# Row statistics moved into the gated FFN, and three small moves in an attention's order of work

## What is computed

```
x = x + L0_xattn(layernorm(x), ctx)     # attention over channels, with a norm over a whole sample
x = x + L0_ffn(layernorm(x))            # fp8 products; gelu(x Wg) * (x Wu), then W_linear
x = x + L1_xattn(layernorm(x), ctx, ctx)
x = x + L1_ffn(layernorm(x))            # eight experts, the two best of each row, weighted by softmax
```

```
qh, kh, vh = q, k, v reshaped to (batch, head, 32, 512)     # q = layernorm(x), k = v = ctx
sm  = softmax(qh^T kh / sqrt(32))                            # 512 x 512 a head
ret = sum over l of sm[q, l] vh[:, l];  x = x + gamma * ret
```

## Time and profile before

| | us |
|---|---|
| median of 3 executions | 750.81 (748.82 to 752.76) |
| the profiled execution | 750.58 |
| its span on the core | 748.8 |
| PE busy in the span | 699.5 (93%) |
| DVE busy | 567.9 (76%) |
| ACT busy | 412.8 (55%) |
| POOL busy | 365.4 (49%) |
| mean granted TensorE clock | 0.995 |

### The profile page before, as it was taken

How to read it: one execution, slowest core, us unless ns; L and a number is a source line. 1 busy time by engine, 2 the same in 40 slices (tenths; PEclk the granted TensorE clock), 3 DMA queues, 4 the chain that set the end, 5 groups by cost and what they waited for, 6 DMA issues and landing times.

```text
span 748.8 us, 16025 instructions
## 1 busy us (share of the span) xinstructions
PE 699.5 (93%) x5065; PEld 307.8 (41%) x5093; DVE 567.9 (76%) x1109; ACT 412.8 (55%) x777; POOL 365.4 (49%) x357
## 2 busy tenths in 40 slices
PE   6999999999999999888999999989988898999995
PEld 2445444444444444322232323222224555555552
DVE  5689999796876869698889998899857565555553
ACT  2554454663646547357788877777776333222221
POOL 5666555113011031364766667776574664343433
PEclk9999999999999999999999999999999999999998
DMA  9999980017365397243344434443555899899895
GB/s 306 392 123 224 320 329 0 1 40 262 115 217 199 120 339 276 67 115 101 95 121 107 114 86 143 137 143 101 164 193 132 169 189 139 125 137 128 132 113 71
DMA packets 114189, 117.62 MB, mean 157 GB/s; under 512 B 54840, under 2 KB 78264, under 8 KB 113856
## 3 DMA queue, kind: packets, MB, share of 16 engines
q1 hardware_dynamic: 103008, 94.48, 43.9%
q0 software_dynamic: 10384, 22.02, 18.1%
q10 hardware_dynamic: 720, 0.13, 0.1%
HBM read 43.61 MB, written 59.56 MB: 138 GB/s over the span
## 4 chain that ended last, share of the span: by engine, by line
PE 17%; DMA 15%; issue 10%; DVE 9%; POOL 2%; SPq 2%; ACT 2%; POOLq 1%; DVEq 0%; ACTq 0%
DMA out<-t_room,t_tag 7%; PE l_b L1579 6%; PE ps_sm L1600 4%; DMA out<-l_pvs,t_tag 4%; DVE l_negm L1827 4%; PE l_pv L1591 3%; DMA out<-l_sums,t_tag 2%; PE l_a L1504 2%; SPq L1060 2%; DVE h_negm L1827 2%; PE l_b L1568 1%; ACT t_room L1734 1%; POOLq L1248 1%; DVE l_rst L1839 1%; DMA h_stack<-h_wide 1%
## 5 line engine op out<-in xcount | busy, mean ns | idle before, releaser
L1734 ACT ACTIVATE t_room<-l_b 128x512 f32<-128x512 f32 x256 | 139.8, 599 | 38.1 <-PE l_b L1579 34.7
L1175 PE MATMUL l_a<-w1h,h_stack 128*128 x312 | 76.5, 314 | 3.0 <-issue 1.7
L1827 DVE TENSOR_REDUCE l_negm<-l_a 128x2 f32<-128x1024 f32 x64 | 75.2, 1219 | 3.6 <-PE l_a L1504 3.1
L1204 ACT ACTIVATE l_stack<-l_stack 128x352 f32<-128x352 f32 x39 | 19.4, 498 | 105.3 <-DVE l_stack L1228 101.7
L1827 DVE TENSOR_REDUCE h_negm<-l_a 128x2 f32<-128x1024 f32 x56 | 65.9, 1220 | 4.9 <-PE l_a L1504 4.6
L1600 PE MATMUL ps_sm<-t_room,ones_f 128*32 128x512 f32 x512 | 66.6, 594 | 2.4 <-ACT l_sums L1745 2.0
L1591 PE MATMUL l_pv<-t_room,l_vt 128*32 128x512 f32 x512 | 66.5, 594 | 0.4 <-issue 0.4
L861 PE MATMUL ps_r<-f_xt,wg 128*128 128x512 fp8e4 x256 | 65.7, 379 | 0.0
L861 PE MATMUL ps_st<-f_xt,wg 128*128 128x512 fp8e4 x256 | 65.7, 379 | 0.0
L1018 POOL TENSOR_TENSOR X<-X,f_y 128x512 f32<-128x512 f32 x15 | 19.4, 1293 | 76.6 <-ACT f_y L915 76.6
L1258 POOL DMA_INDIRECT out<-t_room,t_tag x20 | 31.7, 1585 | 47.7 <-DVE t_room L1243 38.4
(11 more groups left out here) (316 smaller groups left out, 1572.0 us busy)
## 6 DMA issues: line engine op xcount, KB each, us to landing
slots_x<-empty SPq DMA_DIRECT2D x8, 2376.0 KB, 11.2
slots_x<-empty SPq DMA_DIRECT2D x7, 2112.0 KB, 17.4
h_stack<-h_wide SPq DMA_DIRECT2D x96, 64.0 KB
l_stack<-h_wide SPq DMA_DIRECT2D x96, 64.0 KB
...
```

What stands on the lines that cost most here:

```text
L1175: mm = pe.matmul(self.HP[i % 2][:, 0:self.H], T.xt[i % T.AHEAD][:, xp * self.FC + f, :], self.w1[wp][:, bass.ds(e, 1), f * self.H:(f + 1) ...
L1734: act.activation(weights_at(u, c, h)[:, :], B[t % 2][:, :], ACT.Exp, scale=SCALE).then_inc(b_ok, 1)
L1827: dve.tensor_reduce(negm[u % 2][:, 2 * half:2 * half + 2, j], A[half][:, :, :], AX.X, ALU.max, negate=True)\
```

## The change

The statistics of units 0 to 9 are computed in the FFN: those of units 0 to 3 and 4 to 7 at the end of DVE's work in the second and third group, those of 8 and 9 in the last group, at m = 0 and m = 11. mv, veps and rstd get a place for each of the 16 tiles, so a power may take several at once, and the addition of eps too. In the attention, unit u computes the statistics of unit 10 + u as long as there is one (u = 0 to 5), with POOL's power at the same place as before; the step ahead of the loop (that of unit 2) falls away, and POOL's memset of the second stack's row of ones no longer waits for it. `normalise` stands behind maxima(u+2, 1). The adding product is made as four products, each with 32 of the 128 columns of the stationary operand, into four column groups. In unit 1, SP sends the row of maxima of unit 2 ahead of that unit's values.

```diff
--- before.py
+++ after.py
@@ -938,6 +938,7 @@
                         dve.tensor_tensor(EW.w2[1][0:rows, e, cols], stage2[0:rows, cols], EW.w2[0][0:rows, e, cols], ALU.subtract)\
                             .then_inc(lo2_ok, 1)
 
+            SOON_AT = (0, 11)
             LATE = (1, 2, 3, 4, 5, 6, 9, 10, 12, 13, 14, 15)
 
             def group(g, more):
@@ -968,18 +969,24 @@
                         split(2 * g, m - (HC - 6))
                     if not more and m in LATE:
                         split(2 * g + LATE.index(m) // 6, LATE.index(m) % 6)
-                    if not more and m == 0:
-                        F.statistics(dve, X, 0)
+                    if not more and m in SOON_AT:
+                        u = (g - 1) * G + SOON_AT.index(m)
+                        dve.wait_ge(res_ok, u + 1)
+                        F.statistics(dve, X, u, u + 1)
                     if not more and m == 7:
                         F.queries(dve, X, 0)
-                    if not more and m == 11:
-                        F.statistics(dve, X, 1)
+                    if not more and m == SOON_AT[-1]:
+                        F.variances(dve, (g - 1) * G, (g - 1) * G + len(SOON_AT))
                 dve.wait_ge(h8_ok, g * HC + HC)
                 if more:
                     for part in range(6):
                         split(2 * g + 1, part)
                     if g == 0:
                         last.vector(dve, HC)
+                    else:
+                        dve.wait_ge(res_ok, g * G)
+                        F.statistics(dve, X, (g - 1) * G, g * G)
+                        F.variances(dve, (g - 1) * G, g * G)
                 else:
                     for k in range(2 * F.TC):
                         dve.wait_ge(F.a_ps, k + 1)
@@ -1001,12 +1008,12 @@
                     last.gpsimd(pool, last.batches)
                 if not more:
                     pool.wait_ge(res_ok, g * G)
+                    pool.wait_ge(F.rstd_ok, (g - 1) * G)
                     pool.memset(F.stack[F.M0:F.M0 + 1, 0, :, :], 1.0).then_inc(F.set_ok, 1)
                     pool.wait_ge(F.set_ok, 1)
-                    F.power(pool, neg_half, 0)
                     F.low_keys(pool, F.parts, 0)
                     F.low_queries(pool, F.parts, 0)
-                    F.power(pool, neg_half, 1)
+                    F.power(pool, neg_half, (g - 1) * G, F.SOONER)
                 for r in range(G):
                     if not more and r == 2:
                         F.low_keys(pool, F.parts1, 1)
@@ -1016,7 +1023,10 @@
                     pool.wait_ge(y_ok, g * G + r + 1)
                     xr = X[:, bass.ds(g * G + r, 1), :]
                     pool.tensor_tensor(xr, xr, y[r % 2][:, :], ALU.add).then_inc(res_ok, 1)
-
+                if more and g:
+                    F.power(pool, neg_half, (g - 1) * G, g * G)
+
+            assert (NG - 2) * G + 2 == F.SOONER
             groups(pool, group)
 
     return range(ops.stat_ok.num, lo2_ok.num + 1)
@@ -1025,7 +1035,9 @@
 class FirstUnit:
 
 
-    def __init__(self, nc, st, D, DH):
+    SOONER = 10
+
+    def __init__(self, nc, st, D, DH, NT):
         HU, TC = P // DH, D // P
 
         def sb(name, shape, dt=F32):
@@ -1040,7 +1052,7 @@
         parts = [self.wide[:, 2 * k * D:2 * (k + 1) * D].bitcast(BF16).rearrange("p (n d) -> p n d", d=D) for k in range(2)]
         self.parts, self.parts1 = parts
         self.kf, self.qf = self.wide[:, 4 * D:5 * D], self.wide[:, 5 * D:6 * D]
-        self.st6, self.mv, self.veps, self.rstd = sb("st6", [P, 6]), sb("mv", [P, 2]), sb("veps", [P, 1]), sb("rstd", [P, 1])
+        self.st6, self.mv, self.veps, self.rstd = sb("st6", [P, 6]), sb("mv", [P, NT, 2]), sb("veps", [P, NT]), sb("rstd", [P, NT])
         self.negm = sb("negm", [P, HU, TC])
         self.mrow = sb("mrow", [HU * TC, P], BF16)
         self.kf_ok, self.stack_ok, self.row_in, self.set_ok = sem("kf"), sem("stack0"), sem("row0"), sem("set")
@@ -1063,23 +1075,26 @@
     def place_rows(self, sp, stack, mrow, row_in):
         sp.dma_start(stack[self.M0:self.M0 + 1, 1, :, :].rearrange("o h (j t) -> o (h j) t", t=P), mrow[:, :]).then_inc(row_in, 16)
 
-    def statistics(self, dve, X, u):
-        wait(dve, self.rstd_ok, u)
-        dve.bn_stats(self.st6[:, :], X[:, u, :]).then_inc(self.stat_ok, 1)
-        wait_apart(dve, (self.stat_ok, u + 1), (self.qf_ok, u))
-        dve.bn_aggr(self.mv[:, :], self.st6[:, :]).then_inc(self.aggr_ok, 1)
-        dve.wait_ge(self.aggr_ok, u + 1)
-        dve.tensor_scalar(self.veps[:, :], self.mv[:, 1:2], EPS, None, ALU.add).then_inc(self.veps_ok, 1)
+    def statistics(self, dve, X, first, last):
+        for u in range(first, last):
+            wait(dve, self.aggr_ok, u)
+            dve.bn_stats(self.st6[:, :], X[:, u, :]).then_inc(self.stat_ok, 1)
+            dve.wait_ge(self.stat_ok, u + 1)
+            dve.bn_aggr(self.mv[:, u, :], self.st6[:, :]).then_inc(self.aggr_ok, 1)
+
+    def variances(self, dve, first, last):
+        dve.wait_ge(self.aggr_ok, last)
+        dve.tensor_scalar(self.veps[:, first:last], self.mv[:, first:last, 1], EPS, None, ALU.add).then_inc(self.veps_ok, last - first)
 
     def queries(self, dve, X, u):
         dve.wait_ge(self.rstd_ok, u + 1)
         wait(dve, self.ql_ok, u)
-        dve.tensor_scalar(self.qf[:, :], X[:, u, :], self.mv[:, 0:1], self.rstd[:, :], ALU.subtract, ALU.mult).then_inc(self.qf_ok, 1)
-
-    def power(self, pool, neg_half, u):
-        pool.wait_ge(self.veps_ok, u + 1)
-        wait(pool, self.qf_ok, u)
-        pool.tensor_tensor(self.rstd[:, :], self.veps[:, :], neg_half[:, 0:1], ALU.pow).then_inc(self.rstd_ok, 1)
+        dve.tensor_scalar(self.qf[:, :], X[:, u, :], self.mv[:, u, 0:1], self.rstd[:, u:u + 1], ALU.subtract, ALU.mult).then_inc(self.qf_ok, 1)
+
+    def power(self, pool, neg_half, first, last):
+        pool.wait_ge(self.veps_ok, last)
+        pool.tensor_tensor(self.rstd[:, first:last], self.veps[:, first:last], neg_half[:, 0:last - first], ALU.pow)\
+            .then_inc(self.rstd_ok, last - first)
 
     def high_keys(self, act, parts, u):
         act.wait_ge(self.kf_ok, 16 * u + 16)
@@ -1462,8 +1477,12 @@
             for u in range(NU):
                 if u and u + 1 < NU:
                     load_stack(u + 1)
-                    load_values(u + 1)
-                    place_rows(u + 1)
+                    if u == 1:
+                        place_rows(u + 1)
+                        load_values(u + 1)
+                    else:
+                        load_values(u + 1)
+                        place_rows(u + 1)
                 if u == NU - 1:
                     for k in range(2):
                         sp.wait_ge(stack_ok[k], STACKED * (NU // 2))
@@ -1529,7 +1548,10 @@
                 if j == 0:
                     pe.wait_ge(start_ok, 3)
                 pe.wait_ge(b_ok, t - 1)
-                pe.matmul(B[t % 2][:, LOGITS:LOGITS + E], parts_sum[:, :], of_expert[:, :], start=True, stop=True).then_inc(b_ps, 1)
+                for k in range(HU):
+                    of_rows = slice(DH * k, DH * k + DH)
+                    mm = pe.matmul(B[t % 2][of_rows, LOGITS:LOGITS + E], parts_sum[:, of_rows], of_expert[:, :], start=True, stop=True)
+                mm.then_inc(b_ps, 1)
 
             def rank(n, t):
                 N, both = len(BATCHES[n]), boths[n % 2]
@@ -2028,7 +2050,6 @@
                 ht, from_ps = tiles.turned(dve, i)
                 dve.tensor_copy(ht, from_ps).then_inc(tiles.ht_ok, 1)
 
-            F.statistics(dve, X, 2)
             for j in range(EARLY):
                 maxima(1, j)
             dve.wait_ge(gam_ok, 16)
@@ -2060,16 +2081,17 @@
                 if u == NU - 1:
                     first_ends()
                     meeting_table(0, SOON, soon_passed, soon_skipped)
-                if u + 3 == NU - 1:
+                if u == NU - 1 - F.SOONER:
                     dve.wait_ge(x_ok, 1)
-                if u + 3 < NU:
-                    F.statistics(dve, X, u + 3)
+                if u < NU - F.SOONER:
+                    F.statistics(dve, X, F.SOONER + u, F.SOONER + u + 1)
+                    F.variances(dve, F.SOONER + u, F.SOONER + u + 1)
                 if u + 2 < NU:
                     maxima(u + 2, 0)
+                if u + 2 < NU:
+                    maxima(u + 2, 1)
                 if u:
                     normalise(u - 1)
-                if u + 2 < NU:
-                    maxima(u + 2, 1)
                 if u + 3 < NU:
                     F.queries(dve, X, u + 3)
                 for n in range(3):
@@ -2201,8 +2223,7 @@
                         for k in range(2):
                             scatter(*sent_in[u][part], k)
 
-            F.power(pool, neg_half, 2)
-            pool.wait_ge(F.rstd_ok, 3)
+            pool.wait_ge(F.ql_ok, 2)
             pool.memset(stack[1][M0:M0 + 1, 0, :, :], 1.0).then_inc(set_ok, 1)
             pool.wait_ge(set_ok, 2)
             pool.wait_ge(carried_ok, 1)
```

(6 more changed lines are left out.)

## The result

The changed kernel takes 757.99 us (median of 17 runs, 755.66 to 761.99), the kernel before in the same set 752.64 (17 runs). The ratio is 1.0075, with a 95% interval of 1.0058 to 1.0093: 5.6 us slower (4.4 to 7.0), where I had forecast 2.3 faster. The profiled execution took 759.64 us, its span is 757.9, which is 9.1 more than the span of before; it lies 1.6 us above its own median, so the profile shows a somewhat dear execution. Two single executions far from all others, 1006 us of e9 and 2463 us of the kernel before in its set, are left out of the ratios. The lines of the changed kernel are numbered anew: scores for the maxima L1523, transposed rows L1530, adding product L1553, scores L1601, product L1613, ones L1622, ACT's scaling L1762, maxima L1849, fused step L1855, queries L1092, placement L1949 to L1955, POOL's addition L2191.

What follows compares the result with a forecast made beforehand. The prediction took PE's own sequence and the stalls in it as the bound. From the profiled execution it summed 750.58 - 1.1 - 2.6 - 0.8 + 1.5 + 0.7 = 748.3 us, range 744.6 to 752.8.

Steps and rivals of the forecast that it cites:

- What bounds the kernel: In the attention, PE's own order sets a bare unit of about 14.5 us, with stalls on top in certain units.
- Adding product, -2.6: In the attention's logits, four column groups save 0.20 us a unit over 13 units, 2.6 us.
- Fused step, unit 3, -1.1: With the maxima ahead of the fused step, PE's two stalls in unit 3 go: 0.38 + 0.74 = 1.1 us.
- Row, -0.8: At unit 2's start, sending the row before the values shortens PE's 1.65 us stall by 0.8 us.
- Statistics, 0: Statistics moved from the attention into DVE's idle time in the FFN: 0 us gained by themselves.
- the relieved case: Rival: DVE reaches each late chain ahead, the late attention stalls (3.1 us) go; 743.0 us, chance 0.18.
- Fused step in the batch passes, +1.5: In units with batch steps, the fused step behind the maxima lengthens PE's stalls: 0.6 + 0 + 0.6 + 0.3 us.
- Addition meets the placement, +0.7: In batch units, POOL's addition runs beside DVE's placement: between nothing and 2.4 us, taken as 0.7 in all.
- The port rival: Rival: POOL's addition takes the shared port before DVE's queries, 0.96 us more in units 1 to 12; 755.8 us, chance 0.10.

Runs made afterwards that it cites:

- e9: The changed kernel with its three other parts undone, so the moved statistics alone; ratio 1.0021 to the kernel before, 1.6 us slower (0.2 faster to 3.4 slower).
- e3: The kernel before with only the logits' adding product in four column groups; ratio 0.9978, 1.6 us faster (0.2 to 3.0).
- e2: The kernel before with only the fused step moved behind both maxima; ratio 1.0114, 8.6 us slower (6.2 to 10.9).
- e5: The kernel before with the adding product in column groups, the earlier row, and the fused step behind both maxima in loop pass 3 alone; ratio 1.0006.
- e7: As e1, with POOL's low part of the rows held until after DVE's fused step from pass 6 on; ratio 1.0022 to the kernel before.
- e8: The changed kernel with POOL's memset at the end of the third FFN group ahead of the power of four columns; ratio 1.0058 to the kernel before.
- e1: The changed kernel with the fused step put back between the two maxima of unit u+2; ratio 1.0042 to the kernel before.
- e6: The changed kernel with each batch's placement taken ahead of the fused step; ratio 1.0017 to the kernel before.
- e12: The changed kernel with POOL's addition into X held until the placement is through, in the three batch passes; ratio 1.0043 to the kernel before.

## Why the prediction was wrong, by its own steps

- **What bounds the kernel**: right. PE's order sets a bare unit, now 14.28 us; the stage behind does not absorb the loss.
- **Adding product, -2.6**: right in mechanism and within its error: -1.6 (e3), 0.13 to 0.19 a unit in the records. The 60 cycles that the Trainium skill gives each matmul (TensorEngine Tiling (Array Packing), Performance Considerations) would, by my estimate, have made it slower. I misread why not: eight times 60 cycles at 2.4 GHz are 0.20 us, so eight records in 0.21 or 0.22 us do not contradict the page. What fails is the other side of the estimate: two would take 0.05 us, but from the old product's start to the scores' 0.32 us passed, and now 0.25.
- **Fused step, unit 3, -1.1**: half right. Alone (e2) unit 3 is 0.6 shorter; in the changed kernel 0.6 longer. There the earlier row makes POOL later and the queries meet POOL's low part; what share each has was not separated. I had costed each edit by itself and never put the row's into POOL's order.
- **Row, -0.8**: wrong. I followed it to the first scores of unit 2 and no further. The microsecond comes back as a later landing of the next stack: nothing gained alone (ratio 1.0015, its interval on both sides of 1), and with the step of pass 2 in its old place a pause of 2.4 to 2.6 us in four of five kernels (not in e5).
- **Statistics, 0**: right that DVE's load there frees no stall (e9 excludes the relieved case, and e7, without the longer fused step, shows no gain either). Wrong in "POOL stands idle there too": the moved power pushes the memset onto DVE's first cast (+0.6, e8), and the power that left had kept POOL's low part off the fused step.
- **Fused step in the batch passes, +1.5**: for unit 7 I had 0.6, it is 1.5 (1.7 in e2). But e1, with the step back, has 17.00 there too, from POOL's low part (e7, without that, 15.85), so in the changed kernel the 1.5 cannot be put on the step alone. For unit 8 I had 0 since "the missing statistics bring DVE back to PE's pace"; they do not. With the 0.7 us of the step and the 1.6 of the placement one comes to the 2.2 by which unit 12 of e2 is longer; the step's share alone was not measured.
- **Addition meets the placement, +0.7**: this is the step that failed, in its size. I bounded one placement at 1.2 us from a single instruction, 2.4 for two, and went to the low end. But not only the addition stands in line: POOL's cast and subtraction follow at once, and each of the placement's tensor-tensors waits for one of them. That the placements already paid something was right, 0.9 us each; with the change each of the two pays 2.5, so the term is 3.1 us in units 8 and 12 (2.7 with the third, which got shorter), in a chain with no slack. e6 and e12, which take this away in two different ways, remove 3.4 to 3.8 us from each of the two units, the fall of the clock with it.
- **The clock**: missing from the sum. This is the second part of the failure: I priced a longer wait of PE at its own length. At 1.7 to 1.9 us a fall it is nearly half of what units 8 and 12 lost in the profiled execution.
- **The port rival** named the right resource (whichever starts first holds it for its whole instruction; the Trainium skill, SBUF — State Buffer, section SBUF: two separate sides) and the right sign, in the wrong place: the queries won, as I had argued, and the placement behind them lost. By that rule the small instruction ends when the large one does, and the ends above agree to 0.05 us (0.28 for the cast beside the memset). Its time of 755.8 was the nearest of the four, by accident.
